# Layer 1's self-attention: the maxima subtracted by a matmul into the scores' bank, and exponentials that read the bank

## What is computed

```
q = q * cos + rotate_half(q) * sin
k = k * cos + rotate_half(k) * sin
a1 = jnp.einsum('bhqd,bhkd->bhqk', q1, k1) * scale
a2 = jnp.einsum('bhqd,bhkd->bhqk', q2, k2) * scale
...
a1 = a1 + neg
a2 = a2 + neg
p1 = jax.nn.softmax(a1.astype(jnp.float32), axis=-1).astype(x.dtype)
p2 = jax.nn.softmax(a2.astype(jnp.float32), axis=-1).astype(x.dtype)
diff = jax.nn.relu(p1 - lam[None, :, None, None] * p2)
diff = diff / (diff.sum(axis=-1, keepdims=True) + 1e-06)
out = jnp.einsum('bhqk,bhkd->bhqd', diff, v)
```

## Time and profile before

| | |
|---|---|
| median of 3 runs | 869.37 us |
| the profiled execution | 872.1 us, its span 869.7 us |
| mean granted clock of PE | 0.954 |
| PE busy | 786.0 us, 90% of the span |
| DVE busy | 562.0 us, 65% |
| ACT busy | 381.9 us, 44% |
| POOL busy | 238.5 us, 27% |

### The profile page before, as it was taken

The page is one execution under the profiler, slowest core; times in us unless marked ns, Lnnn a source line. Parts: engine busy times, 40 slices in busy tenths (PEclk is TensorE's granted clock), DMA queues, the critical chain, the costliest instruction groups (busy, mean ns, idle before and its releaser), DMA issues. The chain is left out here.

```text
span 869.7 us, 15244 instructions
## 1 busy us (share of the span) xinstructions
PE 786.0 (90%) x5224; PEld 567.6 (65%) x5224; DVE 562.0 (65%) x1299; ACT 381.9 (44%) x847; POOL 238.5 (27%) x296
## 2 busy tenths in 40 slices
PE   5888888999999999998677999989998887999996
PEld 2445454778898999995335556555655536888884
DVE  3798874634333222223787999899996456888864
ACT  1455544333321111110224766666665406888860
POOL 2434430250000000003633333443542321333340
PEclk8999988999999999999899999899999798999999
DMA  9353651284089999863720001001116108999817
GB/s 339 168 211 153 243 194 37 59 299 169 13 282 334 376 377 314 314 209 107 201 86 2 25 2 54 25 33 48 32 46 254 47 37 315 410 410 394 342 60 248
DMA packets 57103, 158.01 MB, mean 182 GB/s; under 512 B 7180, under 2 KB 36748, under 8 KB 51708
## 3 DMA queue, kind: packets, MB, share of 16 engines
q1 hardware_dynamic: 51700, 141.97, 45.1%
q0 software_dynamic: 5328, 15.08, 4.8%
HBM read 114.21 MB, written 42.81 MB: 181 GB/s over the span
## 5 line engine op out<-in xcount | busy, mean ns | idle before, releaser
L1267 PEld LDWEIGHTS ps<-f_xT,f_rg 128*128 128x128 f32 x920 | 113.3, 192 | 6.0 <-DMA f_rg<-w_routed 2.6
L1267 PE MATMUL ps<-f_xT,f_rg 128*128 128x128 f32 x920 | 114.0, 275 | 1.9 <-DMA f_rg<-w_routed 1.9
L1172 DVE TENSOR_TENSOR f_rhT<-f_gate,ps 128x256 f32<-128x256 f32 (+1 forms) x69 | 25.9, 376 | 118.0 <-ACT f_gate L977 79.8
L2074 ACT ACTIVATE b_PX<-ps 128x512 f32<-128x512 f32 x128 | 72.6, 597 | 46.5 <-PE ps L2309 42.9
L1807 DVE TENSOR_REDUCE b_smax<-ps 128x4 f32<-128x1024 f32 x64 | 77.8, 1216 | 15.7 <-PE ps L2285 15.3
L977 ACT ACTIVATE f_gate<-ps 128x256 f32<-128x256 f32 (+1 forms) x69 | 24.1, 349 | 135.0 <-PE ps L1267 135.0
L2602 POOL DMA_INDIRECT y<-f_ys,f_to x47 | 45.1, 959 | 81.6 <-DVE f_to L2680 78.0
L1281 PE MATMUL ps<-f_rd,f_rhT 128*128 128x256 f32 x230 | 62.3, 387 | 0.0
L2309 PE MATMUL ps<-b_Q,b_Cx 100*128 100x256 f32 x256 | 55.9, 327 | 6.3 <-ACT b_PX L2074 6.0
L2309 PEld LDWEIGHTS ps<-b_Q,b_Cx 100*128 100x128 f32 x256 | 41.9, 206 | 26.6 <-ACT b_PX L2074 11.9
L1579 POOL MEMSET b_half<- 128x1 f32 x1 | 0.1, 98 | 213.0 <-POOLq L68 213.0
(11 more groups left out here) (333 smaller groups left out, 1860.9 us busy)
## 6 DMA issues: line engine op xcount, KB each, us to landing
f_rg<-w_routed SPq DMA_DIRECT2D x23, 1280.0 KB
rows<-a_blank SPq DMA_DIRECT2D x16, 1152.0 KB, 7.4
f_rd<-w_routed SPq DMA_DIRECT2D x23, 640.0 KB, 5.4
f_rw<-w_ffn SPq DMA_DIRECT2D x19, 704.0 KB
rw<-w_ffn SPq DMA_DIRECT2D x16, 704.0 KB
later<-w_ffn SPq DMA_DIRECT2D x12, 704.0 KB
f_xs<-rows SPq DMA_DIRECT2D x31, 144.0 KB
f_yk<-y SPq DMA_DIRECT2D x8, 512.0 KB, 8.5
```

The source lines that it names most:

```text
L1267: mm = nc.tensor.matmul(ps[:, u % 4, k * P:(k + 1) * P], rg[b % R_SLOTS][:, off:off + P], xT[b % 2][:, c, :], start=(c == 0), stop=(c == C ...
L2074: nc.scalar.activation(PX[g % RING][:].rearrange("p c m -> p (c m)"), ps[:, RETS + G_TURN[g] % 2, :], ACT.Exp, scale=XSC).then_inc(turn_re ...
```

## The change

DVE now only reduces each bank's maxima, negated, into `mx` as float32r (`greatest`). A new PE step `shift(t, k)` multiplies an identity (`idr`, float32r) with these maxima, each repeated over 64 columns, and adds the product to the bank that holds the scores. ACT's `exps` takes a bank at a time, four per tile, straight from PSUM to `e`. Banks are now free when their exponentials are done, so score(1) and tile 1's projections wait for `exp_ready` instead of `shifted`; tile 1's transposed rows go to bank 3 instead of bank 1. The order of the calls around it changes on DVE, ACT and PE.

```diff
+        idr = sb("idr", [P, P], F32R)
...
-        mx = slots("mx", [P, UNITS * BLK])
+        mx = slots("mx", [P, UNITS, BLK], F32R)
...
+            def greatest(t, k):
+                if t is None:
+                    return
                 dve.wait_ge(scored, t * UNITS + k + 1)
-                sc = ps[:, k % 3, :].rearrange("p (h k) -> p h k", k=SEQ)
-                m = mx[s][:, u * BLK:(u + 1) * BLK]
-                step.done(nc.vector.tensor_reduce(m, sc, AX, ALU.max))
-                step.wait()
-                eu = e[s][:, u].rearrange("p g h k -> p (g h) k")
-                nc.vector.tensor_tensor(eu, sc, bc(m, 2, SEQ), ALU.subtract).then_inc(shifted, 1)
+                nc.vector.tensor_reduce(mx[t % 2][:, k, :], ps[:, k % 3, :].rearrange("p (h k) -> p h k", k=SEQ), AX, ALU.max,
+                                        negate=True).then_inc(max_ready, 1)
...
-                dve.wait_ge(exp_ready, t * B2 + b + 1)
+                dve.wait_ge(exp_ready, t * UNITS + B2 + b + 1)
...
-                shift(e_, 0)
-                shift(e_, 1)
+                greatest(e_, 0)
+                greatest(e_, 1)
                 maxima(b_, 7)
-                shift(e_, 2)
-                shift(e_, 3)
+                greatest(e_, 2)
+                greatest(e_, 3)
                 if e_ == 0:
                     rope(1)
+                maxima(a_, 0)
                 weights(e_, 0)
-                maxima(a_, 0)
                 weights(e_, 1)
...
+            def exps(t, k):
+                if t is None:
+                    return
+                act.wait_ge(shifted, t * UNITS + k + 1)
+                u = k % B2 * JP + k // B2
+                nc.scalar.activation(e[t % 2][:, u].rearrange("p g h k -> p (g h k)"), ps[:, k % 3, :], ACT.Exp, scale=SC
+                                     ).then_inc(exp_ready, 1)
...
                 if e_ == 0:
                     apply_norm(1, 0)
-                    keep_xT(1, 0)
...
                 x_exp(b_, 8)
+                exps(e_, 0)
+                exps(e_, 1)
                 x_exp(b_, 9)
+                exps(e_, 2)
                 x_exp(b_, 10)
-                exps(e_, 0)
+                exps(e_, 3)
+                if e_ == 0:
+                    keep_xT(1, 0)
                 keep_q(a_)
                 keep_max(b_, 3)
-                exps(e_, 1)
...
-                    pe.wait_ge(shifted, t * UNITS + 1)
+                    pe.wait_ge(exp_ready, t * UNITS + 1)
...
+            def shift(t, k):
+
+                if t is None:
+                    return
+                pe.wait_ge(max_ready, t * UNITS + k + 1)
+                nc.tensor.matmul(ps[:, k % 3, :].rearrange("p (h k) -> p h k", k=SEQ), idr[:], bc(mx[t % 2][:, k, :], 2, SEQ),
+                                 start=False, stop=True, skip_group_check=True).then_inc(shifted, 1)
...
+                shift(a_, 0)
                 first_scores(c_, 14)
+                shift(a_, 1)
                 first_scores(c_, 15)
                 if a_ in (0, 1):
                     keep_busy(5)
                 score(a_, 1)
+                second_scores(c_, 9)
+                shift(a_, 2)
+                second_scores(c_, 10)
+                shift(a_, 3)
                 if a_ == 0:
                     turn_xn(1, 0)
...
-                second_scores(c_, 9)
-                second_scores(c_, 10)
                 spread_q(b_)
```

More of the change, by code:

```diff
@@ L1478, in attention1 @@
         scored = sem("scored")
+        max_ready = sem("max_ready")
         shifted = sem("shifted")
@@ L1678, in set_masks @@
                 nc.vector.tensor_copy(idb[:], ident)
+                nc.vector.tensor_copy(idr[:], ident)
                 nc.vector.tensor_copy(causal[:], K[:, K_CAUSAL:K_CAUSAL + SEQ]).then_inc(mask_set, 1)
@@ L1984, in keep_xT @@
                 act.wait_ge(xn_turned[k], t + 1)
-                to, bank = (xT[t % 2], int(t == 1)) if k == 0 else (cT, OUT)
+                to, bank = (xT[t % 2], FIRST * int(t == 1)) if k == 0 else (cT, OUT)
                 nc.scalar.copy(to[:], ps[:, bank, 0:D].rearrange("p (c t) -> p c t", c=C)).then_inc(xT_ready[k], 1)
@@ L2004, in keep_qT @@
                 nc.scalar.copy(qT[t % 2][:].rearrange("p j h q -> p (j h q)"), ps[:, 0, 0:D]).then_inc(qT_ready, 1)
-            def exps(t, b):
+            def exps(t, k):
                 if t is None:
                     return
-                act.wait_ge(shifted, t * UNITS + b + 3)
-                eb = e[t % 2][:, b * JP:(b + 1) * JP].rearrange("p u g h k -> p (u g h k)")
-                nc.scalar.activation(eb, eb, ACT.Exp, scale=SC).then_inc(exp_ready, 1)
+                act.wait_ge(shifted, t * UNITS + k + 1)
+                u = k % B2 * JP + k // B2
+                nc.scalar.activation(e[t % 2][:, u].rearrange("p g h k -> p (g h k)"), ps[:, k % 3, :], ACT.Exp, scale=SC
+                                     ).then_inc(exp_ready, 1)
             def relu(t, b):
@@ L2142, in turn_xn @@
                 pe.wait_ge(xn_ready[k], t + 1)
-                if k == 0 and t == 1:
-                    pe.wait_ge(shifted, 2)
-                elif k == 0:
+                if k == 0 and t != 1:
                     pe.wait_ge(pT_ready[1], t)
-                else:
+                if k == 2:
                     pe.wait_ge(read_cross, t + 1)
-                of, bank = (xn[t % 2], int(t == 1)) if k == 0 else (row[t % 2], OUT)
+                of, bank = (xn[t % 2], FIRST * int(t == 1)) if k == 0 else (row[t % 2], OUT)
                 for c in range(C):
@@ L2158, in project @@
                 pe.wait_ge(xT_ready[0], t + 1)
+                if t == 1:
+                    pe.wait_ge(exp_ready, 2)
                 if t > 1:
@@ L2165, in project @@
                 if t == 1:
-                    pe.wait_ge(shifted, 3)
+                    pe.wait_ge(exp_ready, 3)
                 if t > 1:
@@ L2184, in turn_qk @@
                 if t == 1:
-                    pe.wait_ge(shifted, UNITS)
+                    pe.wait_ge(exp_ready, UNITS)
                 for n in range(2 * JP):
@@ L2396, in _ @@
                     turn_qk(1)
-                    pe.wait_ge(exp_ready, 1)
+                    pe.wait_ge(exp_ready, UNITS)
                     keep_busy(6)
```

2 lines of the change are left out of this document (removed).

## The result

The changed kernel takes **911.13 us**, the median of four runs (909.49 to 911.83), against 869.37 us of the kernel before: a ratio of 1.048, 95% interval [1.0446, 1.0519]. (A fourth run of the kernel before took 4093.03 us and is left out.) That is 42 us slower where 33 were forecast, and inside the range. The profiled execution took 911.7 us with a span of 909.9.

What follows compares the result with a forecast made beforehand. The prediction took DVE as the full engine bounding the loop over tiles. Seven tiles at 4.5 us, plus 2.6 in tile 0, less 0.7 behind tile 7, gave 33.4 us on 869.4: 903 us, range 888 to 917.

Steps and rivals of the forecast that it cites:

- The chain of small steps up to maxima(a, 1): From a tile's first maximum, late score(1) delays later steps until DVE stands 3.7 us before maxima(a, 0); 4.5 us later overall.
- the dear end of that bound: New float32r matmuls on PE might each cost up to 0.3 us more than 0.24, adding about 0.9 us per tile.
- The block by POOL: On DVE, the second weights' product, now neighbour to the first weights, is blocked by POOL: 1.0 us more per tile.
- the 4.5 us: Delay per tile from first maximum to maxima(a, 1), said to pass to the next tile because DVE has little idle time.
- The rival without the block: POOL does not block the second weights: 3.5 us per tile, 896 us in all; chance 0.14.
- PE's clock: Rival: PE, nearly idle before first_scores 4 and 5, drops its clock longer: 1.85 us per tile, 916 us; chance 0.16.
- The ramp: Tile 0 loses 2.6 us through the late keep_xT(1, 0) and projection; tile 1 loses 4.5 us like later tiles.
- Behind tile 7: No scores follow and DVE is less full, so 0.7 us of that tile's 4.5 us is taken back.
- The faster rival: DVE's relief of 2.8 us per tile shows and its waits don't, PE allowing 1.9 per tile: 856 us; chance 0.06.
- 28.4 us of matmuls per tile: In the faster case, PE's 27.4 us of matmuls and 1.0 more were taken as the least time per tile.

Runs made afterwards that it cites:

- e3: Kernel before, subtractions kept on DVE, with only DVE's order changed to maxima(a, 0), weights(0), weights(1): 891.35 us, ratio 1.0257.
- e1: Changed kernel with DVE's order put back to weights(0), maxima(a, 0), weights(1), all else kept: 887.12 us, ratio 1.0234.
- e6: e1 with the first two subtractions on PE and exponentials on ACT moved ahead of second_scores and x_exp 7 and 8: 880.96 us.
- e7: e6 with spread_q, first_scores 0 and 1, keep_q, pick and take moved earlier, and idle work added in the ramp: 872.11 us, ratio 1.0031.
- e9: e7 with bank 7 as fourth scores bank in tiles 0 and 1, and tile 1's transposed rows moved forward: 864.79 us, ratio 0.998.
- e5: e4 with the second weights moved behind maxima(a, 1), so the two weights are not neighbours: 902.82 us, ratio 1.0393.
- e8: e4 with products L1759 and L1761 left out of every tile's second weights (result wrong): 899.57 us, ratio 1.0335.
- e4: Changed kernel with 13 unused bfloat16 matmuls per tile on PE ahead of first_scores 4: 902.61 us, ratio 1.0406.

## Why the prediction was right, and by how much it was off

- **The chain of small steps up to maxima(a, 1) held within 0.2 us.** Counted from the tile's first maximum: score(1) forecast at 3.25 us, measured 3.27; maxima 2 at 4.93, measured 4.95; first_scores(b, 0) at 9.20, measured 9.09; maxima(a, 0) at 9.95, measured 9.87, with 3.62 us of idle time before it instead of 3.7; maxima(a, 1) at 15.6, measured 15.46. The float32r product was 0.22 us, near the 0.24 taken, so the dear end of that bound fell away.
- **About half of the loss is DVE's order, with what it does to the clock; the other half is the longer way through three engines.** e3 has 22 to 25 us of loss without any new product, and e1 gets 22 to 24 back with all of them in place. The 20 us left in e1 are not the price of the products' work as such: e6, e7 and e9 keep the four products, change the order, and reach the time of the kernel before.
- **The block by POOL was there but put on the wrong path.** It was forecast as 1.0 us, and measured as 0.92 in each tile; e5 and e8 show that taking it away returns 0.2 to 0.4 us. The forecast passed the 4.5 us at maxima(a, 1) on to the next tile through DVE; what passes on is PE's wait for POOL at turn_probs. The sum came out right since POOL's own chain is late by as much: weights(0) start 11.01 us after the first maximum (605.85) where the earlier trace rows had 6.43, 4.6 us later, and POOL's differences with them. That the two paths are late by nearly the same is luck in the size; that the cause of both is weights(0) standing behind maxima(a, 0) was forecast. The rival without the block, 3.5 us per tile, was therefore priced wrong: by e5 and e8 it is 34.37 - 30.27 = 4.1 and 34.21 - 30.27 = 3.9.
- **PE's clock was not a rival but a part of the sum.** The forecast gave it a case of its own with 1.85 us per tile. It came in every tile from 2 to 6, at 6.6 / 5 = 1.3 us. What the forecast held against it, that DVE sets the pace behind that point, does not hold: from turn_probs on PE does (15.1 us with no wait at full clock), so PE can't make up there what it loses. In the tile above, first_scores 4 fall into a stretch at 0.50 (the 1.2 GHz level) behind the 3.28 us in which PE stood, by the table by stretch:

```profile
611.40:614.80 3.40, 3.23 (x21) 1.81 (x22) 3.30 (x8) 0.99 (x2) 2.42 (x3) 0.50 0.02 5
```

  e4 gives its price, 6.6 to 8.5 us in all, most or all of the distance from 903 to 911.
- **The ramp was mis-sized.** Forecast 2.6 + 4.5 for tiles 0 and 1, measured 4.7 + 7.2, 11.8 in all. Its two kinds of wait are on DVE, ended by PE:

```profile
425.06 1.29 DVE L1745 TENSOR_REDUCE b_mx<-ps 128x8 fp32r<-128x512 f32 x2 [4.78 <-PE ps L2221]
429.22 0.49 DVE L1727 TENSOR_TENSOR b_qk<-ps,K 128x320 f32<-128x320 f32 x1 [2.87 <-PE ps L2164]
...
455.02 1.29 DVE L1745 TENSOR_REDUCE b_mx<-ps 128x8 fp32r<-128x512 f32 x2 [5.44 <-PE ps L2221]
```

  The step counted tile 1's projection (the 2.87) and left out that in tiles 0 and 1 nothing lies over the way from maximum to product, exponential and score(1): 4.78 and 5.44 us of idle DVE. keep_busy, which stands ahead of score(1) there, ran at half clock on top of it, 2.36 us for its five products (1.25 in the kernel before), by PE's timeline and the table by stretch:

```profile
450.23 2.36 PE L2381 MATMUL ps<-b_causal,b_idb 128*128 128x512 bf16 x5
```

```profile
440.70:454.40 13.70, 11.82 (x40) 4.23 (x39) 5.70 (x14) 2.95 (x7) 2.53 (x3) 0.50 0.11 32
```

  Tile 1 was counted like the others; e9, which takes that wait away, shortens this stretch by 7.7 us against e7. How much of the ramp's loss is the wait and how much PE's clock was not taken apart.
- **Behind tile 7** 4.1 us more, forecast 3.8.
- **The faster rival** (856) needed DVE's new waits to stay under 2.8 us. e7 brings them to 3.6 - 1.1 = 2.5, and the time only returns to that of before, because PE has taken the place of DVE: the 15.1 us behind turn_probs did not shrink by anything that DVE was spared. The bound that the forecast put there, 28.4 us of matmuls per tile, was too low as a time: at 28.95 busy the tile takes 30.47.

## What to carry to other kernels

Work taken from the full engine pays only as far as its queue still has something to do at the same moments: look first at what the removed instructions were lying over, and which instruction next in the queue now has to wait in the open. An engine's place in a handshake (maximum, product, exponential, bank free) is longer on three engines than on one, so move the order of the calls behind it, as e6, e7 and e9 do, before judging the change. And price a stall by what the engine behind it waits for: a blocked instruction whose result goes to an engine that is still busy costs little. Here the place to read was the one wait of PE, at turn_probs, behind which the tiles of all these kernels take the same 15.1 us at full clock.

## What the runs showed of the hardware beside that

A product of two 128x8 tiles in SBUF on DVE, 0.17 us alone, can last as long as several instructions of POOL in a row. In e9's ramp, on DVE and on POOL:

```profile
425.51 2.03 DVE L1762 TENSOR_TENSOR b_w<-b_w,b_lamt 128x8 f32<-128x8 f32 x1
```

```profile
424.67 0.95 POOL L1588 DMA_INDIRECT later<-y,dest  x1 [0.30 <-issue]
425.64 0.86 POOL L1615 TENSOR_TENSOR b_qk<-b_qk,b_rot 128x320 f32<-128x320 f32 x1
426.46 1.04 POOL L1625 TENSOR_TENSOR b_e<-b_e,b_w 128x512 f32<-128x512 f32 x1
```

DVE's product begins 0.13 us ahead of POOL's first one by the profile and ends at 427.54, with POOL's second one (427.50). So by these times it lay beside both of POOL's products, which started after it. POOL's DMA_INDIRECT still ran until 425.62, so that may be what held it first. This is one place, seen in one profile; what decides there was not tried.
